# Decoder with two cross attentions: the values product of a key tile as one matmul per head of 512 queries, between the third and the fourth scores product

## The reference, cut to what matters

```python
q = (x @ Wq.T).reshape(b, s, 16, 16)            # 16 heads of 16 features
k, v = ...                                       # from the context
scores = einsum('bhsd,bhed->bhse', q, k) * 16**-0.5
attn = softmax(where(mask == 0, -inf, scores))   # the second layer has no mask
out = einsum('bhse,bhed->bhsd', attn, v)
y = out.reshape(b, s, 256) @ Wo.T
```

## Time and profile before

| what | value |
|---|---|
| runs | 2182.59, 2183.37, 2188.12 us; median 2183.37 us |
| profiled execution | 2184.47 us, of which the span is 2182.4 us |
| busy share of the span | PE 83%, DVE 50%, ACT 44%, POOL 12% |
| instructions | 45725 |
| values product (L1161) | 4352 matmul records, 379 ns median |
| exponentials (L1270) | 1088, 598 ns median |
| wide items on DVE (L1321) | 512, 992 ns median |
| narrow items on DVE (L1318) | 128, 1226 ns median |

### The profile page before, as it was taken

One profiled execution on the slowest core, in us unless ns is written; L12 is line 12 of the kernel. 1 busy time (PEld: TensorE's weight loads), 2 busy tenths in 40 slices (PEclk: granted clock), 3 DMA queues, 4 the chain that ended last, 5 costly groups with the idle time before them and its releaser, 6 DMA issues.

```text
span 2182.4 us, 45725 instructions
## 1 busy us (share of the span) xinstructions
PE 1814.0 (83%) x16832; PEld 921.7 (42%) x16833; DVE 1100.5 (50%) x1481; ACT 950.6 (44%) x1663; POOL 263.4 (12%) x215
## 2 busy tenths in 40 slices
PE   6889968999799685766999999999997179999980
PEld 2334423444244232322455455455443156666650
DVE  4663348777211324437888788788741211121115
ACT  3331235777411413321778678688693012122110
POOL 4134010001300200220000000000002500000005
PEclk9989988999899897887999999999997589999995
DMA  8101051110100000362000000000005410000003
GB/s 324 47 32 47 0 105 39 33 32 17 55 0 0 5 0 6 42 104 66 10 10 18 11 10 17 11 18 10 3 3 228 169 32 29 29 24 29 29 27 111
DMA packets 64172, 97.14 MB, mean 45 GB/s; under 512 B 11505, under 2 KB 56753, under 8 KB 62075
## 3 DMA queue, kind: packets, MB, share of 16 engines
q1 hardware_dynamic: 60922, 86.21, 13.7%
q0 software_dynamic: 3072, 8.39, 1.2%
HBM read 65.20 MB, written 28.97 MB: 43 GB/s over the span
## 4 chain that ended last, share of the span: by engine, by line
PE 56%; issue 5%; DVE 4%; POOL 3%; ACT 3%; DMA 1%; SPq 0%; DVEq 0%; ACTq 0%; POOLq 0%
PE ps L517 9%; PE ps L1812 9%; PE ps L1118 8%; PE ps L1186 8%; PE ps L1161 8%; PE ps L1827 5%; PE ps L1469 2%; DVE arena L1321 2%; PE ps L441 1%; PE ps L1223 1%; POOL rows_in L1921 1%; POOL arena L1926 1%; PE ps L1820 1%; PE ps L1171 1%; DMA qparts<-arena 1%
## 5 line engine op out<-in xcount | busy, mean ns | idle before, releaser
L1270 ACT ACTIVATE arena<-ps 128x512 f32<-128x512 f32 x1088 | 596.5, 602 | 179.5 <-PE ps L1186 145.9
L1321 DVE TENSOR_REDUCE arena<-ps 128x1 f32<-128x802 f32 (+1 forms) x512 | 494.4, 989 | 70.1 <-PE ps L1118 68.1
L517 PE MATMUL ps<-arena 128*128 (+1 forms) x832 | 382.2, 620 | 73.1 <-DVE arena L1610 23.2
L1186 PE MATMUL ps<-arena 100*32 100x512 bf16 x4352 | 386.7, 384 | 9.6 <-issue 5.7
L1118 PE MATMUL ps<-arena 97*32 97x400 bf16 (+2 forms) x5120 | 355.5, 354 | 46.9 <-DVE arena L1321 18.4
L1161 PE MATMUL ps<-arena 128*32 128x256 f32 x4352 | 332.1, 380 | 1.5 <-ACT arena L1270 0.9
L517 PEld LDWEIGHTS ps<-arena 128*128 128x128 f32 x832 | 163.9, 199 | 290.7 <-issue 290.7
L1812 PE MATMUL ps<-arena 128*128 x608 | 198.9, 470 | 29.2 <-ACT arena L1880 29.2
L1118 PEld LDWEIGHTS ps<-arena 97*32 97x32 bf16 x5120 | 129.8, 97 | 200.9 <-DVE arena L1321 59.8
L1161 PEld LDWEIGHTS ps<-arena 128*32 128x32 f32 x4352 | 133.8, 111 | 100.8 <-issue 7.3
L2007 DVE TENSOR_TENSOR arena<-ps,arena 128x352 f32<-128x352 f32 x76 | 40.0, 526 | 269.3 <-ACT arena L1887 197.2
(11 more groups left out here) (187 smaller groups left out, 1456.1 us busy)
## 6 DMA issues: line engine op xcount, KB each, us to landing
arena<-in_experts_w SPq DMA_DIRECT2D x8, 2176.0 KB, 16.5
arena<-qparts SPq DMA_DIRECT2D x192, 64.0 KB, 2.3
qparts<-arena SPq DMA_DIRECT2D x48, 128.0 KB, 2.0
rows_in<-arena SPq DMA_DIRECT2D x1, 5120.0 KB, 35.9
arena<-in_ctxT SPq DMA_DIRECT2D x3, 1664.0 KB, 9.7
kparts<-arena SPq DMA_DIRECT2D x24, 208.0 KB, 2.4
arena<-kparts SPq DMA_DIRECT2D x12, 416.0 KB, 14.3
arena<-rows_in SPq DMA_DIRECT2D x38, 128.0 KB, 2.1
```

Of the source, the lines that this page charges most:

```text
L517: ins = eng.matmul(out, w[:, k, m * P:(m + 1) * P], x[:, k, tok(c)], start=k == 0, stop=k == ktiles - 1)
L1186: ins = eng.matmul(ring_bank(r)[j:j + 32], Kst[0:ROWS, at_head(g * HG + h), kt * P + j:kt * P + j + 32], Qst[0:ROWS, g, h, :], start=True, ...
L1270: eng.activation(probs[:, keys_of(u, kt) % 2, h, :], ring_bank(r), ACT.Exp, bias=0.0).then_inc(ring_read.sem, 1)
L1321: eng.tensor_reduce(MX[:, par, heads[0] * QT + q, n % 2:n % 2 + 1], got, AX.XY, ALU.max).then_inc(slot_free.sem, 1)
```

## The change

The values product of a key tile is no longer cut in two. Its four matmuls take all 512 queries, in the place where cut 0 stood, and the step after the scores of head 3 is gone.

```diff
-            PV_CUTS = 2
+            PV_CUTS = 1
             PVW = CH // PV_CUTS
...
                     yield ("scores", kt, 2)
                     if has_values:
                         yield ("pv",) + values + (0,)
                     if mine[1] is not None:
                         yield ("item",) + mine[1]
                     yield ("scores", kt, 3)
-                    if has_values:
-                        yield ("pv",) + values + (1,)
                     if kt == AT_DEN and u > 0 and window:
                         yield ("den",)
                     if mine[2] is not None:
                         yield ("item",) + mine[2]
```

## The result

The changed kernel takes 2243.39 us (median of 4 runs, 2242.89 to 2250.42) against 2182.98 us of the kernel before in the same comparison: a ratio of 1.028 with a 95% interval of 1.0253 to 1.0306. The profiled execution is the slowest of the four, 2250.42 us with a span of 2248.5.

The account below looks back on a forecast made before the run. PE was taken to bound the wide attention, busy 544.59 of 566 us. Waits of 35 + 14.6 + 8 + 2 + 6.2 = 65.8 us on the profiled 2184.5 gave 2250 us, range 2222 to 2268.

Parts of the forecast that it names:

- The values product: Per key tile: one piece takes 0.87 us, as two cuts did; no difference, halved weight loads worth nothing.
- The item after a tile of three: Wide attention: PE waits 0.48 us for a slot, 0.42 more; with the turn's 0.39, 2.5 a unit, 35 us.
- a longer product for nothing: Rival at the values product: matmul count, not columns, sets its time; 0.43 us a tile, 2131 us; chance 0.03.
- The scores after a tile of two: Wide attention: head 2 waits 0.18 us for head 3's bank, 81 times, 14.6 us.
- Tiles without items: Both attentions: such a tile takes 2.27 us instead of 1.95; 25 by 0.32 is 8 us.
- The narrow attention: Head 2's bank waits of 0.08 us, 3.4 in all, and a turn 0.2 later per unit, 2.8: together 6.2 us.
- So I expect no lower clock: PE, wide attention: longest new hole, 1.66 us, is close to the turn's existing 1.27, so the clock stays.
- holes in other places and a lower clock: Signs of a wrong prediction: PE holes elsewhere than forecast, or a lower clock in the wide attention.
- items behind DVE: Sign in the waits: items (L1116) waiting for DVE rise by some 30 us.
- scores behind ACT: Sign in the waits: scores (L1184) waiting for ACT rise by some 25 us.
- only the slots wait: Rival: ACT answers in under 1.00 us, so bank waits fall away; 39 us slower, 2224 us; chance 0.10.
- the first eight tiles of the unit before the last: Wide attention: four waits of 0.18 us and three of 0.42 there add 2 us.

Follow-up runs that it names:

- e5: The changed kernel run once more, nothing altered: 2244.41 us, ratio 1.0255 to the kernel before.
- e1: The kernel before, still with two cuts, its second cut moved directly behind the first: 2241.75 us, ratio 1.0244.
- e2: The changed kernel, with the second item of a wide tile of three moved ahead of the product: 2200.83 us, ratio 1.0067.
- e6: The changed kernel, with waits in an untaken branch ahead of the second layer's loop in PE's program: 2236.97 us, ratio 1.0223.
- e4: The changed kernel, with the two cuts given back to the 25 key tiles without items: 2233.44 us, ratio 1.0217.
- e8: The kernel before with two cuts; in the wide attention the turn moved later and some items ahead of cuts: 2172.25 us, ratio 0.9928.

## Why the prediction was right, and where a step was off

Forecast 2250, measured 2243.39: the sign and the mechanism held; 65.8 us were added up and 60.4 came. That the sum came so close is luck: the bank waits were put some 12 us too high, and the loop's return, which the prediction does not have, cost about as much (9.7 us in e5, 12.9 in the profiled execution).

- *The values product*: 0.87 said, 0.86 measured. Right; e1 sets one piece against two cuts in one place.
- *The item after a tile of three*: a wait of 0.48 said, 0.49 measured, and 1.62 for the slot again. The turn was to wait 1.66 and waits 1.60. 2.5 us a unit said; e2 takes away 2.79, of which some 0.06 a tile had been waited for before already. Right. The rival of a longer product for nothing falls with the 0.86 of the line above.
- *The scores after a tile of two*: **the term that was mis-sized**. The answer time of a bank, "0.52 + 0.66 = 1.18", took its 0.52 from the scores of 1323.76. These are of head 0, whose exponential also waits for the values product; the bank that is waited for is head 3's. That answers in 0.45, so the answer is 1.11 and the wait 0.10, for 0.18 said. 81 by 0.10 is 8 us and not 14.6; a tile without items took 2.18 and not 2.27; and the 3.4 us of the narrow attention, where head 2 comes after 1.10, fall away. That is some 12 us too many.
- *Tiles without items*: 8 us said, 3.5 measured. A tile in the middle of such a row costs 0.23, but a whole row less than its tiles by 0.23: from the last item to the last product of denominators the wide attention took 40.91 us before (1605.42 to 1646.33) and 44.20 after (1667.18 to 1711.38), the narrow one 21.67 (538.42 to 560.09) and 21.83 (543.43 to 565.26). For its seven such tiles the prediction had 2.2 us, and 0.2 came.
- *The narrow attention*: 8.4 us said, with its seven tiles without items; 5.4 measured (from the first load of queries to the load of the next stage, 241.1 to 246.5 us), and 4.4 in e5 (245.5). The turn came as said: it starts 1.95 after its item, which starts 0.43 later, where it was 2.17, so 14 by 0.2 are 2.8. The rest is a wait that the prediction does not have. The ring starts over in each unit, so that head 1 of a unit's first key tile takes the bank that head 3 of the tile before had; within a unit it is mostly head 2 that does so. In the change head 1 is due there 0.88 after head 3, and starts after 1.10, 0.22 late (rows below; the first holds heads 3 and 0, the second heads 1 and 2, and an item stands between). This stands in 8 places, in the profiled execution and in e5, and in none before: 1.7 us. 2.8 and 1.7 make the 4.4 of e5; the last 1.0 of the other execution was not followed.

```profile
429.56 0.61 PE L1184 MATMUL ps<-arena 100*32 100x512 bf16 x8
...
430.66 0.62 PE L1184 MATMUL ps<-arena 100*32 100x512 bf16 x8
```

- *"So I expect no lower clock"*, and no word on the loop's return: **wrong**. The step held at the turns, with one exception in the profiled execution: behind the turn at 1074.63 the window from 1070 to 1080 has a clock of 0.83, which e5 has not. It failed at the two returns. Taking a plain unit's 2.97 off what the two units with a return gained (9.75 and 9.07), they cost 12.9 us more in the profiled execution and 9.7 in e5, of which 9.1 and 7.1 are the holes and the rest steps at half clock behind them. Nothing in the rows of before told of it, since the holes there were 2.73 and 3.00. The prediction had named holes in other places and a lower clock as signs that it is wrong, and at the returns both came.

For the wide attention of the profiled execution this closes: 61.8 us are seven plain units (20.6), two with the output product (5.6), two with a return (18.8), the first (4.7) and what comes after the last load (12.0). In e5, which lies at the median, the stage is 55.5 longer; with the 4.4 of the narrow attention that is 59.9, and its profiled execution is 59.9 us over that of the kernel before.

Of the signs, the waits are hard to read: items behind DVE rose by 22 us on PE and 38 on PEld for the 30 said, scores behind ACT by 5 and 44 for the 25 said. The distances between steps tell more.

The rival "only the slots wait" (2224) is not borne out: the bank wait is 0.10, between its nothing and the 0.18 of the forecast. With what was measured, the corrected sum is 35 + 8 + 3.5 + 1.7 + 4.5 = 53, or 2237 us (1.7 for the first eight tiles of the unit before the last, 4.5 for the narrow attention without its tiles that have no items). The loop's return carries it to what was measured: 2237 + 9.7 is 2247, less 1.8 for the products 2245, where e5 has 2244.41. And e6, which has the change and the short holes, is at 2236.97.

What would have shown the size beforehand: to compare the exponentials' start with that of their own scores for all four heads, not for one.

## What to carry to other kernels

Cutting a long step of the bound engine costs nothing here (0.01 us a tile) and sets the pace at which the other engines get work: between two uses of the same buffer should lie at least its answer time, 1.62 us for a slot that DVE reduces and 1.11 for a bank that ACT reads, measured from start to start. Before a long step is put in one place, write down these distances in the new order; every one that falls below the answer time is a wait, and its size is the difference. And take an answer time from the very instruction that is waited for: one of its neighbours had another wait, and that alone put some 12 us too many into the sum.

## What was not expected of the hardware

The return of a loop on PE costs 2.7 to 7.5 us, depending on where the loop lies in the program. In the table the holes of two returns are 5.4 to 6.3 us in five runs (before, e1, e4, e6, e8) and 12.8 to 14.8 in the six others; between e5 and e6, 128 instructions that never run move it from one group to the other. What fills the hole is not shown by an experiment, and the rows name no one that PE waits for. One thing goes with its length: the queue that the page calls "instruction" moved one packet of 16 KB in each of the ten short holes (2.7 to 3.2 us) and two in each of the twelve long ones (6.1 to 7.5). That fits a PE that waits for its own program after the jump; the packets do not name their engine, so it stays argued. Behind the long ones of the change PE ran at a granted clock of 0.50 for some microseconds; behind the short ones of before it did not, and in e6 it did from its third step on. Any change that adds or takes away instructions of PE can so gain or lose some 7 us of this kernel's time, 0.3%, whatever it was meant to do; a verdict of that size needs the holes at the returns read beside it.
